# GpSimd adds the two key chunks of a head's last 132 queries, and the row sums on TensorE read 256 columns per head instead of 388

## The chip, the cores and the metric

The kernel runs on one core of a Trainium2 chip. The metric is device time in microseconds (us) of one execution. The engines are named as in the profile: PE is TensorE's matmul stream and PEld its weight loads, DVE is VectorE, ACT is ScalarE, POOL is GpSimd, and SP issues most of the DMAs.

## What is computed

A pre-norm transformer layer for 32 batches of 256 tokens of width 128, all in float32 at the interface. The attention has 16 heads of 64, rotary embedding, and 4 persistent keys and values in front of the 256 own ones, so each head has 260 keys. Cut to what matters here:

```python
scores = einsum('bhid,bhjd->bhij', q, k) * scale
scores = where(j <= i + 4, scores, min)          # i query, j key, 4 persistent keys
attn = softmax(scores, axis=-1)                   # exp, divided by its sum over the keys
out = einsum('bhij,bhjd->bhid', attn, v)          # then @ w_out.T and the residual
x = x + ffn(layernorm(x))                         # a gated scan over the batches
```

The step that the change touches is the sum over the keys in the softmax.

## The kernel before

**Tiles.** A batch has 8 pairs of heads, called s = 0 to 7. Keys lie on the 128 partitions in two chunks: chunk 0 holds keys 0 to 127 and meets all 256 queries; chunk 1 holds keys 128 to 255 and, by the causal mask, meets only queries 124 to 255 (Q1 = 124). The last four keys are handled apart in `prob_end`. So the exponentials of a head are 256 + 132 = 388 columns, and `prob` is `[128, 4 slots, 2 heads, 388]` in float32, with slot s % 4.

**Order of the work.** Every engine runs one outer loop over j and inside it eight steps s, an order written out by hand. Several batches are in flight: batch j is projected, batch j-1 goes through scores and attention, batch j-2 is normalised and projected out, batch j-3 goes through the feed-forward gates. In a step s the work runs as follows.

- PE: `project(j, s)` into the one bank `ps_proj` (L953), then work of other batches, `scores_for_max` (L985), `scores_t(j-1, s)` (L1007, L1010), `attend(j-1, s-1)` (L1044), and after it, where s is 2, 4, 7 and 0, the sums of four heads: `sums(j-1, 0)`, `sums(j-1, 1)`, `sums(j-1, 2)` and, in step 0 of the next j, `sums(j-2, 3)` (L1063). In steps 5 and 6 stands `project_out(j-2)`, four groups n = 0 to 3 (L1080), in step 3 and 7 a transpose of the row maxima (L993), and in step 0, right after `project(j, 0)`, `transpose_xn` (L1095).
- DVE: `rotate` (L752, L753), `maxima` (L763), in steps 4 and 5 the four `divide` (L799) that multiply by 1/sum, in step 6 `residual` (L804) and at its end `c_lo` (L843).
- SP: two DMAs that swap neighbouring partitions of `rope_b` into `rope_c`; in step 2 the DMAs that store 1/sum and spread it over the partitions (`linv_scratch`, `rinv`).
- POOL, the engine of the change: `rope_add(j, s-1)` (L385) waits for the swap's DMA; in step 7 `rstd(j-2)` (L393 to L399, four small operations on 2 columns); then `causal(j-1, s)`, two selects that zero what lies above the diagonal (L376, L378); in step 1 also `factors`.
- ACT: `exp(j-1, s)` (L521), `hi(j, s-1)` (L506, waits for `rope_add`), `raw_copy(j-1, s-1)` (L544), and in step 7, behind them, `second_norm(j-2)` (L600), which waits for `rstd` and whose result `xn` is what `transpose_xn` waits for.

**The sums.** Four heads r use four groups of 32 columns of the PE array at the same time. A float32 matmul is run as two instructions, so each chunk takes two rounds of four matmuls. The weights `ones_sum` are 1/256 in the column of the head's group.

Of the kernel before, what the change touches and what calls it, by code (L numbers as in the profile page):

```python
# [5 lines left out]
NB, NT, D = 32, 256, 128  # L6
NH, DH, NPM = 16, 64, 4
DI = NH * DH
P = 128
NPAIR = NH // 2  # L10
QT = NT // P
NKEY = NT + NPM
NEND = NKEY - 2 * P
Q1 = P - NPM
QE = NT - NEND
SCOL = NT + (NT - Q1)
CHUNKS = [(0, 0, 0), (1, Q1, NT)]
# [23 lines left out]
def wait(eng, sem, count):  # L41

    if isinstance(count, int) and count <= 0:
        return
    eng.wait_ge(sem, count)


def build(nc, x, x_last, w_qkv_t, w_out_t, norm_w, pm_k, pm_v, ffn_w, ffn_b, bo_row, consts_f32, consts_cast,
          out):
    f32, f16, bf16 = mybir.dt.float32, mybir.dt.float16, mybir.dt.bfloat16  # L50
    ALU = mybir.AluOpType
# [6 lines left out]
    with ctx:  # L58
        def sb(name, shape, dt):
            return ctx.enter_context(nc.sbuf_tensor(name, shape, dt))  # L60

        def sem(name):
# [62 lines left out]
        top = sb("top", [P, 2, QT, P], f32)  # L125
        masked = sb("masked", [P, 2, SW0 + NKEY], bf16)
        prob = sb("prob", [P, 4, 2, SCOL], f32)

# [15 lines left out]
        c2 = sb("c2", [P, NT], f32)  # L146
        c_hi = sb("c_hi", [P, NT], f16)
        c_lo = sb("c_lo", [P, NT], f16)
        cf = sb("cf", [P, QT * D], f32)
        linv_dram = nc.dram_tensor("linv_scratch", [2, 32, 2, NT], f32, kind="Internal").ap()  # L150
        v_end_dram = nc.dram_tensor("v_end_scratch", [P, DI], f32, kind="Internal").ap()

# [11 lines left out]
            "casts_act casts_dve casts_pool end_xn end_tr end_hi end_done ve_ready ve_copied ve_stored "  # L164
            "h_stats h_rstd h_xn h_tr h_hi_done h_lo_done "
            "qk_proj qk_read swapped0 swapped1 rope_sum hi_done sm_ready max_done top_tr top_copied "
            "st_ready exp_done causal_done pv_ready raw_done sum_ready linv_done linv_stored spread0 spread1 norm_done y_ready x1_done "
            "v_ready v_done v_end sx_done sx_rstd xn_ready xt_ready xt_hi_done xt_lo_done gate_ready gate_read c_hi_done state_done "
            "end_exp end_summed end_added k_end_done lin_ready pre_done cf_ready cf_done fin_sum fin_sum_pool fin_tanh fin_out fin_out_pool stored "
            "dve_tick pool_tick dve_pro dve_s dve_h dve_b dve_c pool_h pool_b").split()}  # L170
# [21 lines left out]
        def real(b):  # L192

            return not isinstance(b, int) or 0 <= b < NB
# [141 lines left out]
        @block.gpsimd  # L336
        def _(pool):
            G = nc.gpsimd
            G.memset(expo[:, :], -0.5).then_inc(S["casts_pool"], 1)
            G.memset(top[:, :, :, :], 0.0).then_inc(S["casts_pool"], 1)  # L340
            G.memset(h_hi[:, :, 0:NPM], 0.0).then_inc(S["casts_pool"], 1)
            G.memset(h_lo[:, :, 0:NPM], 0.0).then_inc(S["casts_pool"], 1)
            G.memset(bo_one[:, :], WS).then_inc(S["casts_pool"], 1)
            G.memset(eps[:, :], EPS_LN).then_inc(S["casts_pool"], 1)
            G.memset(minus[:, :], -1.0).then_inc(S["casts_pool"], 1)
            G.memset(one_e2[:, :], 1.0 + EPS_RMS).then_inc(S["casts_pool"], 1)
            G.memset(e1_e2[:, :], EPS_LN * EPS_RMS).then_inc(S["casts_pool"], 1)
            G.memset(prob_end[:, :, :, :, :], 0.0).then_inc(S["casts_pool"], 1)
            G.memset(prob_end_sum[:, :, :], 0.0).then_inc(S["casts_pool"], 1)
            G.memset(v_end[:, :], 0.0).then_inc(S["casts_pool"], 1)  # L350

            def factors(n, count, base):


                v, u = sh_mv[:, 0:n, 1], sh_u[:, 0:n]
                pool.wait_ge(S["h_stats"], count)
                G.tensor_tensor(u, v, one_e2[:, 0:n], ALU.mult).then_inc(S["pool_h"], 1)
                pool.wait_ge(S["pool_h"], base + 1)
                G.tensor_tensor(u, u, e1_e2[:, 0:n], ALU.add).then_inc(S["pool_h"], 1)
                G.tensor_tensor(sh_m[:, 0:n], sh_mv[:, 0:n, 0], minus[:, 0:n], ALU.mult).then_inc(S["pool_h"], 1)  # L360
                pool.wait_ge(S["pool_h"], base + 3)
                G.tensor_tensor(sh_r[:, 0:n], u, expo[:, 0:n], ALU.pow).then_inc(S["pool_h"], 1)
                pool.wait_ge(S["pool_h"], base + 4)
                G.tensor_tensor(sh_m[:, 0:n], sh_m[:, 0:n], sh_r[:, 0:n], ALU.mult).then_inc(S["h_rstd"], 1)

            pool.wait_ge(S["casts_pool"], 12)
            factors(QT + 1, 1, 0)

            def causal(bj, s):


                pool.wait_ge(S["exp_done"], NPAIR * bj + s + 1)
                G.sem_inc(S["pool_tick"], 1)
                c0 = prob[:, s % 4, :, 0:P]
                c1 = prob[:, s % 4, :, NT:NT + P]
                G.affine_select(out=c0, in_=c0, compare_op=ALU.is_ge, fill=0.0, base=NPM,  # L376
                                pattern=[[0, 2], [1, P]], channel_multiplier=-1)
                G.affine_select(out=c1, in_=c1, compare_op=ALU.is_ge, fill=0.0, base=0,  # L378
                                pattern=[[0, 2], [1, P]], channel_multiplier=-1).then_inc(S["causal_done"], 1)

            def rope_add(j, s):

                wait(pool, S["st_ready"], NPAIR * (j - 1) + s + 1)
                pool.wait_ge(swapped[s % 2], 32 * (NPAIR // 2 * j + s // 2 + 1))
                G.tensor_tensor(qk[:, s, :].rearrange("p (u n) -> p u n", u=2)[:, :, 0:NT],  # L385
                                rope_a[:, s % 4, :].rearrange("p (u n) -> p u n", u=2),
                                rope_c[:, s % 2, :].rearrange("p (u n) -> p u n", u=2),
                                ALU.add).then_inc(S["rope_sum"], 1)

            def rstd(cj):  # L390

                pool.wait_ge(S["sx_done"], cj + 1)
                G.tensor_tensor(sx_b[:, :], sx_mv[:, :, 1], eps[:, 0:QT], ALU.add).then_inc(S["pool_b"], 1)  # L393
                wait(pool, S["xn_ready"], cj)
                G.tensor_tensor(sx_m[:, :], sx_mv[:, :, 0], minus[:, 0:QT], ALU.mult).then_inc(S["pool_b"], 1)
                pool.wait_ge(S["pool_b"], 3 * cj + 2)
                G.tensor_tensor(sx_r[:, :], sx_b[:, :], expo[:, 0:QT], ALU.pow).then_inc(S["pool_b"], 1)
                pool.wait_ge(S["pool_b"], 3 * cj + 3)
                G.tensor_tensor(sx_m[:, :], sx_m[:, :], sx_r[:, :], ALU.mult).then_inc(S["sx_rstd"], 1)  # L399

            def body(j, p):
                a, b, c = real(j), real(j - 1), real(j - 2)
                for s in range(NPAIR):
                    if s == 0 and b:
                        rope_add(j - 1, NPAIR - 1)
                    if s >= 1 and a:
                        rope_add(j, s - 1)
                    if c and s == 7:
                        rstd(j - 2)
                    if b:  # L410
                        causal(j - 1, s)
                    if s == 1 and real(j + 1):
                        factors(QT, j + 2, POOL_H * (j + 1))

            iterations(nc.gpsimd, body)


            def fin_add(g):
                G.tensor_tensor(fin_pre(g), fin_pre(g), over_batches(cf[:, :]), ALU.add).then_inc(S["fin_sum_pool"], 1)

            def fin_res(g):
                pool.wait_ge(S["fin_tanh"], g + 1)
                G.tensor_tensor(fin_x(g), fin_x(g), fin_pre(g), ALU.add).then_inc(S["fin_out_pool"], 1)

            pool.wait_ge(S["cf_done"], 1)
            pool.wait_ge(S["x1_done"], NB)
            fin_add(FIN_POOL[0])
            for i in range(1, len(FIN_POOL)):
                fin_add(FIN_POOL[i])
                fin_res(FIN_POOL[i - 1])  # L430
            fin_res(FIN_POOL[-1])
# [479 lines left out]
        def _(pe):  # L911
# [142 lines left out]
            def sums(bj, g):  # L1054

                if g == 0:
                    wait(pe, S["linv_done"], bj)
                if g == 2:
                    wait(pe, S["x1_done"], bj)
                for kc, q0, c0 in CHUNKS:  # L1060
                    for r in range(4):
                        slot = (2 * g + r // 2) % 4
                        last = T.matmul(ps_sum[32 * r:32 * r + 32, q0:NT], ones_sum[:, g, :],  # L1063
                                        prob[:, slot, r % 2, c0:c0 + NT - q0],
                                        start=(g == 0 and kc == 0), stop=False, skip_group_check=True)
                if g == 3:
                    pe.wait_ge(S["end_summed"], bj + 1)
                    for r in range(4):
                        last = T.matmul(ps_sum[32 * r:32 * r + 32, QE:NT], ones_end[:, r % 2, 32 * r:32 * r + 32],
                                        prob_end_sum[:, r % 2, :], start=False, stop=True, skip_group_check=True)  # L1070
                last.then_inc(S["sum_ready"], 1)
# [244 lines left out]
```

## Time and profile before

| | |
|---|---|
| median of 3 runs | 1206.99 us (1204.7 to 1209.58) |
| the profiled execution, time | 1204.28 us |
| its span in the profile | 1202.5 us |
| PE busy | 1136.8 us (95%) |
| DVE busy | 942.5 us (78%) |
| ACT busy | 684.7 us (57%) |
| POOL busy | 655.0 us (54%) |

A time in the views below is counted from the start of the span. Between the span and the execution's own time lie 1.8 us. A busy PE is a modelled figure: matmuls overlap, so the start of the next one says more than the end of this one.

### The profile page before, as it was taken

The numbers are of one execution on the slowest core, as the hardware profiler recorded it, in microseconds if no ns is written. First come the engines' busy times: TensorE is split into PE (matmuls) and PEld (weight loads), VectorE is DVE, ScalarE is ACT, GpSimd is POOL, SyncE is SP. The second block draws the span as 40 slices with busy tenths as digits, with TensorE's granted clock in tenths as the row PEclk, the third lists the DMA queues.
The fourth block names the chain that finished last, engine by engine and source line by source line (L and its number), as shares of the span: only waits on it lengthen the run. The fifth ranks groups of instructions, "written<-read, shape, count | busy, mean of one in ns | idle before, by whom it ended". The sixth has DMA issues, their size and how long they took to land.

```text
span 1202.5 us, 36709 instructions
## 1 busy us (share of the span) xinstructions
PE 1136.8 (95%) x13099; PEld 802.8 (67%) x13099; DVE 942.5 (78%) x3302; ACT 684.7 (57%) x1474; POOL 655.0 (54%) x1082
## 2 busy tenths in 40 slices
PE   3889999999999999999999999999999999999981
PEld 2556767667776766777677677767667777766661
DVE  5677888888877888787878878877788878788636
ACT  3555565656555566655656665565555565565533
POOL 3544555556555555655555556555556556555425
PEclk8899999999999999999999999999999999999995
DMA  5222333332233333233333323333332333333204
GB/s 200 86 83 79 108 104 112 107 108 83 84 104 98 116 106 109 70 96 106 99 115 109 107 73 92 105 108 108 104 97 78 98 108 95 112 103 97 65 10 140
DMA packets 77990, 119.80 MB, mean 100 GB/s; under 512 B 13041, under 2 KB 35954, under 8 KB 77682
## 3 DMA queue, kind: packets, MB, share of 16 engines
q1 hardware_dynamic: 68722, 111.18, 30.7%
q10 hardware_dynamic: 9088, 6.29, 1.8%
q8 instruction: 105, 1.72, 0.6%
q14 instruction: 75, 0.61, 0.2%
HBM read 41.53 MB, written 8.78 MB: 42 GB/s over the span
## 4 chain that ended last, share of the span: by engine, by line
PE 76%; DVE 6%; DMA 5%; ACT 4%; issue 4%; POOL 3%; SPq 2%; DVEq 0%; ACTq 0%; POOLq 0%
PE bank_pv L1044 13%; PE bank_st L1007 12%; PE bank L953 12%; PE bank_sum L1080 8%; PE bank L971 6%; PE bank_sum L1063 6%; PE bank_sm L985 5%; DMA rope_c<-rope_b 4%; PE bank_st L1010 3%; PE bank L1166 2%; PE bank L1168 2%; ACT xn L600 2%; PE bank_sm L993 2%; POOL qk L385 2%; PE bank L1095 1%
## 5 line engine op out<-in xcount | busy, mean ns | idle before, releaser
L385 POOL TENSOR_TENSOR qk<-rope_a,rope_c 128x512 f32<-128x512 f32 x256 | 336.0, 1312 | 269.7 <-DMA rope_c<-rope_b 264.5
L763 DVE CUSTOM_DVE_ANT_0 masked<-bank_sm,mask_q 128x132 bf16<-128x132 f32 (+1 forms) x1024 | 307.6, 356 | 43.5 <-PE bank_sm L985 42.9
L521 ACT ACTIVATE prob<-bank_st 128x776 f32<-128x776 f32 x256 | 208.5, 814 | 160.0 <-PE bank_st L1010 159.2
L752 DVE TENSOR_TENSOR rope_a<-bank,cos 128x512 f32<-128x512 f32 x256 | 174.1, 680 | 125.1 <-PE bank L953 116.2
L1007 PE MATMUL bank_st<-qk 64*128 64x256 f32 (+1 forms) x2048 | 239.4, 326 | 0.1
L376 POOL TENSOR_SCALAR_AFFINE_SELECT prob<-prob 128x256 f32<-128x256 f32 x256 | 113.9, 445 | 227.5 <-ACT prob L521 226.4
L1044 PE MATMUL bank_pv<-prob,v_sb 128*64 128x256 f32 (+1 forms) x2048 | 224.7, 340 | 2.2 <-POOL prob L378 1.8
L506 ACT ACTIVATE qk_h<-qk 128x512 f16<-128x512 f32 x256 | 160.1, 625 | 98.0 <-POOL qk L385 96.9
L1007 PEld LDWEIGHTS bank_st<-qk 64*128 64x128 f32 x2048 | 154.8, 188 | 31.7 <-issue 0.8
L753 DVE TENSOR_TENSOR rope_b<-bank,sin 128x512 f32<-128x512 f32 x256 | 173.7, 679 | 0.0
L1044 PEld LDWEIGHTS bank_pv<-prob,v_sb 128*64 128x64 f32 x2048 | 124.5, 136 | 72.7 <-issue 31.4
L953 PE MATMUL bank<-h_hi,w_hi 128*128 128x256 f16 x512 | 143.7, 281 | 2.6 <-DVE rope_b L753 1.8
L953 PE MATMUL bank<-h_hi,w_lo 128*128 128x256 f16 x512 | 142.0, 277 | 0.0
L953 PE MATMUL bank<-h_lo,w_hi 128*128 128x256 f16 x512 | 141.8, 277 | 0.0
L1080 PE MATMUL bank_sum<-wo_sb,raw 128*128 128x128 f32 x1024 | 127.2, 277 | 3.2 <-DVE raw L799 3.2
L1080 PEld LDWEIGHTS bank_sum<-wo_sb,raw 128*128 128x128 f32 x1024 | 121.0, 192 | 11.8 <-DVE raw L799 9.0
L1010 PE MATMUL bank_st<-top_t,sel_shift 64*128 64x256 bf16 (+1 forms) x1024 | 126.4, 243 | 0.0
L378 POOL TENSOR_SCALAR_AFFINE_SELECT prob<-prob 128x256 f32<-128x256 f32 x256 | 116.5, 455 | 0.0
L1063 PE MATMUL bank_sum<-prob,ones_sum 128*32 128x256 f32 (+1 forms) x2048 | 110.6, 334 | 0.0
L553 ACT ACTIVATE v_sb<-bank 128x512 f32<-128x512 f32 x128 | 76.5, 597 | 59.5 <-PE bank L971 59.4
L799 DVE SCALAR_TENSOR_TENSOR raw<-rinv,raw 128x512 f32<-128x512 f32 x124 | 93.7, 796 | 5.7 <-DMA rinv<-linv_scratch 5.7
L544 ACT ACTIVATE raw<-bank_pv 128x256 f32<-128x256 f32 x256 | 94.9, 371 | 0.5 <-PE bank_pv L1050 0.5
(190 smaller groups left out, 1712.5 us busy)
## 6 DMA issues: line engine op xcount, KB each, us to landing
rope_c<-rope_b SPq DMA_DIRECT2D x512, 128.0 KB, 2.1
rinv<-linv_scratch SPq DMA_DIRECT2D x124, 256.0 KB, 4.5
out<-x_sb SPq DMA_DIRECT2D x16, 256.0 KB, 2.5
linv_scratch<-linv SPq DMA_DIRECT2D x62, 64.0 KB, 2.0
x_sb<-x ACTq DMA_DIRECT2D x28, 128.0 KB, 4.8
pre<-w_qkv_t ACTq DMA_DIRECT2D x1, 1024.0 KB, 5.5
v_sb<-pm_v SPq DMA_DIRECT2D x64, 8.0 KB
v_end<-v_end_scratch SPq DMA_DIRECT2D x64, 8.0 KB
```

The lines of the kernel that those rows point to most:

```text
L385: G.tensor_tensor(qk[:, s, :].rearrange("p (u n) -> p u n", u=2)[:, :, 0:NT], rope_a[:, s % 4, :].rearrange("p (u n) -> p u n", u=2), rope ...
L506: A.activation(qk_h[:, s, :].rearrange("p (u n) -> p u n", u=2)[:, :, 0:NT], qk[:, s, :].rearrange("p (u n) -> p u n", u=2)[:, :, 0:NT], A ...
L521: A.activation(prob[:, s % 4, :, :], ps_st[:, :, 0:SCOL], ACT.Exp).then_inc(S["exp_done"], 1)
L752: V.tensor_tensor(rope_a[:, s % 4, :], proj_bank(j, s)[:, :], cos[:, :], ALU.mult)
L753: V.tensor_tensor(rope_b[:, s % 2, :], proj_bank(j, s)[:, :], sin[:, :], ALU.mult).then_inc(S["qk_read"], 1)
L763: ins = V.tensor_tensor_reduce(masked[:, e, c0:c0 + n], ps_sm[:, e, c0:c0 + n], mask_q[:, c0:c0 + n], 1.0, LOWEST, ALU.add, ALU.max, top[: ...
L953: last = T.matmul(proj_bank(j, s)[:, u * NT:(u + 1) * NT], W[q][:, col:col + P], H[p][:, par, NPM:NKEY], start=(i == 0), stop=(i == 2))
L1007: T.matmul(ps_st[:, e, c0:c0 + NT - q0], qk[OWN[e], s, NT + kc * P:NT + (kc + 1) * P], qk[OWN[e], s, q0:NT], start=True, stop=False)
L1010: last = T.matmul(ps_st[:, e, c0:c0 + NT - q0], sel_shift[OWN[e], s, :], top_t[OWN[e], s // 4, q0:NT], start=False, stop=True)
L1044: last = T.matmul(ps_pv[OWN[e], q0:NT], v_sb[:, kc, col:col + DH], prob[:, s % 4, e, c0:c0 + NT - q0], start=(kc == 0), stop=(kc == 1))
L1063: last = T.matmul(ps_sum[32 * r:32 * r + 32, q0:NT], ones_sum[:, g, :], prob[:, slot, r % 2, c0:c0 + NT - q0], start=(g == 0 and kc == 0), ...
L1080: last = T.matmul(ps_sum[:, NT + q * D:NT + (q + 1) * D], raw[:, par, s, q * P:(q + 1) * P], wo_sb[:, s, :], start=(alone and s == 0 and q ...
```

## The change

`prob_add` is new on POOL, right behind `causal` in every step. It writes the sum of the two chunks for queries 124 to 255 into the new buffer `prob_2`, after a wait for the sums that last read the slot, and a wait for POOL's own selects. `sums` then runs two parts: queries 0 to 123 from `prob` (chunk 0 alone has keys for them), and queries 124 to 255 from `prob_2`. It waits for `prob_added`. The number of matmuls stays. `attend` still reads `prob`. `cf`, used only at the very end, is laid over `th` to make room.

```diff
+        prob_2 = sb("prob_2", [P, 4, 2, NT - Q1], f32)
...
-        cf = sb("cf", [P, QT * D], f32)
+        cf = th[:, 0, :]
...
+            def prob_add(bj, s):
+
+                wait(pool, S["sum_ready"], 4 * bj + (s - 4) // 2 + 1)
+                pool.wait_ge(S["causal_done"], NPAIR * bj + s + 1)
+                G.tensor_tensor(prob_2[:, s % 4, :, :], prob[:, s % 4, :, NT:SCOL], prob[:, s % 4, :, Q1:NT],
+                                ALU.add).then_inc(S["prob_added"], 1)
+
...
                     if b:
                         causal(j - 1, s)
+                        prob_add(j - 1, s)
...
-                for kc, q0, c0 in CHUNKS:
+                pe.wait_ge(S["prob_added"], NPAIR * bj + 2 * g + 2)
+                for part, (q0, q1) in enumerate(((0, Q1), (Q1, NT))):
                     for r in range(4):
                         slot = (2 * g + r // 2) % 4
-                        last = T.matmul(ps_sum[32 * r:32 * r + 32, q0:NT], ones_sum[:, g, :],
-                                        prob[:, slot, r % 2, c0:c0 + NT - q0],
-                                        start=(g == 0 and kc == 0), stop=False, skip_group_check=True)
+                        src = prob_2[:, slot, r % 2, :] if part else prob[:, slot, r % 2, 0:Q1]
+                        last = T.matmul(ps_sum[32 * r:32 * r + 32, q0:q1], ones_sum[:, g, :], src,
+                                        start=(g == 0 and part == 0), stop=False, skip_group_check=True)
```

## Rows read from the trace of the kernel before

**Rows 1.** The page's head: span, then busy time of each engine.

```profile
span 1202.5 us, 36709 instructions
PE 1136.8 (95%) x13099; PEld 802.8 (67%) x13099; DVE 942.5 (78%) x3302; ACT 684.7 (57%) x1474; POOL 655.0 (54%) x1082
```

**Rows 2.** Waits: engine and line waiting <- releaser: us in total, times, longest.

```profile
POOL qk L385 <- DMA rope_c<-rope_b: 264.5, 129, 8.4
POOL prob L376 <- ACT prob L521: 226.4, 157, 3.9
...
PEld bank L1095 <- ACT xn L600: 14.3, 31, 1.1
...
PEld bank_sum L1080 <- DVE raw L799: 9.0, 18, 0.8
...
PEld bank_pv L1044 <- POOL prob L378: 2.3, 3, 1.2
```

**Rows 3.** Groups of instructions by form: out<-in shapes xcount | busy us, mean ns.

```profile
L385 POOL TENSOR_TENSOR qk<-rope_a,rope_c 128x512 f32<-128x512 f32 x256 | 336.0, 1312 | 269.7 <-DMA rope_c<-rope_b 264.5 <-ACT prob L521 2.7 <-PE bank_st L1010 1.8
...
L378 POOL TENSOR_SCALAR_AFFINE_SELECT prob<-prob 128x256 f32<-128x256 f32 x256 | 116.5, 455 | 0.0
...
L1063 PE MATMUL bank_sum<-prob,ones_sum 128*32 128x256 f32 x1024 | 81.8, 391 | 0.0
...
L1063 PEld LDWEIGHTS bank_sum<-prob,ones_sum 128*32 128x32 f32 x2048 | 53.4, 109 | 40.4 <-issue 17.1
L1063 PE MATMUL bank_sum<-prob,ones_sum 128*32 128x132 f32 x1024 | 52.3, 276 | 0.0
```

**Rows 4.** Timeline of PE around the end of step 7: start us, us, what.

```profile
634.83 0.86 PE L1063 MATMUL bank_sum<-prob,ones_sum 128*32 128x256 f32 x16
635.63 0.28 PE L953 MATMUL bank<-h_hi,w_hi 128*128 128x256 f16 x1
...
636.18 0.27 PE L953 MATMUL bank<-h_lo,w_hi 128*128 128x256 f16 x1
636.56 0.44 PE L1095 MATMUL bank<-ident_f,xn 128*128 128x128 f32 x2
```

**Rows 5.** Timeline of POOL in the same steps 6 and 7.

```profile
631.90 0.41 POOL L378 TENSOR_SCALAR_AFFINE_SELECT prob<-prob 128x256 f32<-128x256 f32 x1
632.27 1.29 POOL L385 TENSOR_TENSOR qk<-rope_a,rope_c 128x512 f32<-128x512 f32 x1
...
634.12 0.71 POOL L397 TENSOR_TENSOR sx_r<-sx_b,expo 128x2 f32<-128x2 f32 x1
634.91 0.19 POOL L399 TENSOR_TENSOR sx_m<-sx_m,sx_r 128x2 f32<-128x2 f32 x1
```

**Rows 6.** Timeline of ACT in step 7 of the same batch.

```profile
634.13 0.82 ACT L521 ACTIVATE prob<-bank_st 128x776 f32<-128x776 f32 x1 [0.51 <-PE bank_st L1010]
...
635.37 0.38 ACT L544 ACTIVATE raw<-bank_pv 128x256 f32<-128x256 f32 x1
635.63 0.87 ACT L600 ACTIVATE xn<-x_sb,sx_m,sx_r 128x128 f32<-128x128 f32 x2
```

**Rows 7.** Timeline of DVE at the end of step 6, same batch.

```profile
632.58 1.26 DVE L843 SCALAR_TENSOR_TENSOR c_lo<-c,c_hi 128x256 f16<-128x256 f32 x1
```

**Rows 8.** All instructions of DVE line 843: duration ns min/median/max.

```profile
L843 DVE SCALAR_TENSOR_TENSOR c_lo<-c,c_hi x32: 390/1268/1373, 141.3 to 1178.5; 128x256 f16<-128x256 f32 x32
```

**Rows 9.** Timeline of POOL in steps 6 and 7, another batch.

```profile
806.16 0.41 POOL L378 TENSOR_SCALAR_AFFINE_SELECT prob<-prob 128x256 f32<-128x256 f32 x1
807.86 1.29 POOL L385 TENSOR_TENSOR qk<-rope_a,rope_c 128x512 f32<-128x512 f32 x1 [1.29 <-DMA rope_c<-rope_b]
...
810.32 0.20 POOL L399 TENSOR_TENSOR sx_m<-sx_m,sx_r 128x2 f32<-128x2 f32 x1
```

**Rows 10.** Timeline of PE in that batch, step 0 of the next j.

```profile
811.48 0.44 PE L1095 MATMUL bank<-ident_f,xn 128*128 128x128 f32 x2 [0.76 <-ACT xn L600]
```

**Rows 11.** Timeline of POOL, ACT and DVE in steps 4 and 5, an early batch.

```profile
200.76 1.28 POOL L385 TENSOR_TENSOR qk<-rope_a,rope_c 128x512 f32<-128x512 f32 x1 [4.01 <-DMA rope_c<-rope_b]
...
202.07 0.63 ACT L506 ACTIVATE qk_h<-qk 128x512 f16<-128x512 f32 x1 [2.75 <-POOL qk L385]
...
203.37 0.48 DVE L698 SCALAR_TENSOR_TENSOR h_lo<-bank,nw,h_hi 128x256 f16<-128x256 f32 x1 [1.34 <-ACT h_hi L460]
```

More of the change, by code:

```diff
@@ L166, in build @@
             "qk_proj qk_read swapped0 swapped1 rope_sum hi_done sm_ready max_done top_tr top_copied "
-            "st_ready exp_done causal_done pv_ready raw_done sum_ready linv_done linv_stored spread0 spread1 norm_done y_ready x1_done "
+            "st_ready exp_done causal_done prob_added pv_ready raw_done sum_ready linv_done linv_stored spread0 spread1 norm_done y_ready x1_done "
             "v_ready v_done v_end sx_done sx_rstd xn_ready xt_ready xt_hi_done xt_lo_done gate_ready gate_read c_hi_done state_done "
```

## The prediction

> **What bounds the kernel now.** I read the page's head first: PE is busy for 95% of the span, DVE for 78%, POOL for 54% [rows 1]. PE's stream is therefore what has to get shorter, and a shorter stream is worth its full length only where PE is not about to wait for something. So the next view is the waits. POOL waits 264.5 us for the swap's DMA and 226.4 us for the exponentials [rows 2]: 491 us over 256 steps, 1.9 us per step, so on average it has room. PE itself waits for little, but one entry comes back in 31 of the 32 batches: the weight load of `transpose_xn` (L1095) waits for `xn` from ACT, 14.3 us in all. A second, `project_out` behind `divide`, comes in 18 batches or groups, 9.0 us; the third, `attend` behind the selects, has 3 cases and 2.3 us [rows 2]. In each batch there are thus one or two places at which another chain is as long as PE's own. What the change is worth is decided there. For the first place I went to the timelines of one ordinary batch [rows 4 to 7] and of one in which POOL was late [rows 9, 10].
>
> **What PE saves.** A group of sums is four rounds of four matmuls, now of 256, 256, 132 and 132 columns, then of 124, 124, 132 and 132. A group and what follows it lie 0.80 us apart (634.83 to 635.63) [rows 4]. A matmul of 256 columns lasts 391 ns, one of 132 columns 276 ns [rows 3]; the fixed part is the same, so a shortened round gives back 115 ns, two of them 0.23 us. A round can also not be shorter than the weight load of the next, 109 ns [rows 3], which holds 124 columns at about the price of 132 and leaves a little more in the first round. I take 0.22 us a group, between 0.20 and 0.23. There are 2048 / 16 = 128 groups: 28 us gross, 2.3%, or 0.88 us a batch. The added wait for `prob_added` costs nothing in itself: the last add needed by `sums` comes one whole step ahead of it, as the select does now, and the selects stop PE 3 times only [rows 2].
>
> **What the add costs on POOL.** No row shows it. A TENSOR_TENSOR on 512 columns takes 1312 ns on average [rows 3] and 1.28 us undisturbed [rows 11]; one on 2 columns takes 0.19 [rows 5]. That is 2.1 ns a column, and for 2 x 132 = 264 columns 0.19 + 0.55 = 0.75 us (rounded). The bounds: not below a select on 256 columns, 0.455 us [rows 3], and not above the 512-column add, 1.31 us. The nearest by kind, two inputs, is the latter, and the line between 2 and 512 columns carries the 0.75. The wait for POOL's own selects is priced as the one in `rstd`: L397 ends at 634.83 and L399 starts at 634.91, 0.08 us [rows 5]. So 0.83 us are inserted after each `causal`, 212 us in all, and POOL comes to about 867 us, 72%. In most steps the 1.9 us of waiting cover it.
>
> **Where it is not covered: step 7.** After `causal(6)` ends (631.90 + 0.41 = 632.31) POOL starts `rope_add(6)` at once (632.27) and then `rstd`, which ends at 634.91 + 0.19 = 635.10 [rows 5]. ACT could start `xn` from then on, and does at 635.63, behind `raw_copy` [rows 6]. PE's projection has its last matmul at 636.18 and `transpose_xn` starts at 636.56 [rows 4]; it waits for `xn`. How much later may `rstd` be? The other batch answers. There the swap was late, `rope_add` began 807.86 - 806.57 = 1.29 us after the select, `rstd` ended at 810.52, 3.95 us after the select instead of 2.79, and PE stood 0.76 us before L1095 [rows 9, 10] instead of 636.56 - 636.45 = 0.11 [rows 4]. So 1.16 us more on POOL became 0.65 us on PE: the slack is 0.51 us. With the add in between, `rope_add` starts about 0.80 us later. A second thing happens there: `c_lo` on DVE, with two inputs in SBUF, asks at 632.58 and lasts 1.26 us, to just after the end of `rope_add` [rows 7]; alone it takes 0.39 [rows 8]. The two engines shut each other out. In the new order either `rope_add` goes first, and `rstd` ends 0.80 + 2.83 = 3.63 us after the select (2.83 is 635.10 - 632.27), or `c_lo` slips in for the rest of its work, about 0.28 us with what overlaps taken off 0.14, and then it is 0.83 + 0.14 + 2.66 = 3.63 again (2.66 is the late batch's 810.52 - 807.86). Both are 0.84 us over the 2.79 of now. Less 0.51 of slack, `transpose_xn` is 0.33 us late in each batch. The work of `xn` starts from `exp(7)`, which itself waits for the scores (634.13, 0.51 <-PE) [rows 6], that is, from a point before `sums(2)`. So the 0.22 us that `sums(2)` saves in step 7 only lengthens the wait for `xn` and is lost in every batch.
>
> The Trainium skill ("SBUF — State Buffer", who interferes with whom) says that a VectorE instruction with two SBUF inputs and a GpSimd instruction that reads SBUF exclude each other for the whole instruction; the trace agrees, with 390 ns against a median of 1268 ns for the same line [rows 8]. By this rule the new add would also hold up `divide`, which is priced as a rival below.
>
> **Where it is half covered: steps 4 to 6.** `rope_add(3)` waits 4.01 us for a swap that queues behind the spreading of 1/sum; ACT waits 2.75 us for it, and DVE 1.34 us for `h_hi` behind that [rows 11]; then come `maxima`, `divide` and `project_out`. This chain starts from the inverse in step 1, before `sums(0)` and `sums(1)`. PE waited for a `divide` 18 times [rows 2]; I count these as 18 batches in which the chain is as long as PE's stream, and there the 0.44 us of `sums(0)` and `sums(1)` are lost too. In the other 13 they are kept. What POOL adds does not lengthen this chain: the add after `causal(3)` lies inside the 4.01 us.
>
> **The sum.** 13 batches keep three groups and pay the delay: 0.66 - 0.33 = 0.33 us gained each, 4.3 us. 18 keep one group: 0.22 - 0.33 = 0.11 us lost each, 2.0 us. The last batch gives 0.2. The span goes from 1202.5 to about 1200 us, the profiled execution from 1204.28 to 1201.8, and the median of the runs, 2.7 us above it, from 1206.99 to 1204.5 us. The smaller buffer for `cf` moves nothing: it is written after the last batch. A measurement of this kernel can tell about 0.5%, 6 us, from no change.
>
> **Rivals.**
>
> 1. *The gain comes through.* The chain in steps 4 to 6 has slack that the 18 waits hide (they are short), or the add is cheaper. With the delay of 0.33 and three groups kept in all 31 batches it is 31 x 0.33 = 10 us: 1197. If the add costs only the lower bound, 0.455, the insertion is 0.54 and the delay 0.04: 31 x 0.62 = 19 us, 1188. For it: POOL's large idle time. Against it: the idle time is not in step 7 [rows 5]. Chance 0.32.
> 2. *POOL's chain takes over in step 7: slower.* The mean gain that can be kept is (13 x 0.66 + 18 x 0.22) / 31 = 0.40 us a batch; the delay passes that once the insertion is above 0.83 + 0.07 = 0.90 us. At the upper bound, 1.31 + 0.08 = 1.39 us, the delay is 0.89 and the loss 31 x 0.49 = 15 us: 1222. At 1.0 us for the add it is 0.18 x 31 = 6 us, 1213. For it: PE waits at this place in all batches already. Against it: the line through two sizes gives 0.75. Chance 0.15.
> 3. *The add shuts out `divide`.* If one add of 0.75 us stands ahead of the last `divide` in step 5 in the 18 tied batches, `project_out` is that much later: 18 x 0.75 = 13 us less the 2 us gained, 1218. Against it: after `causal(4)` there is `rope_add` in the same place already, and a shorter instruction may even help. Chance 0.08.
> 4. *About even*, the forecast: 0.45.
>
> **How the numbers follow.** The time is that of the likeliest case, 1204.5 us; its own range is 1201 to 1212. For 8 in 10 I reach down to 1190, which takes in most of rival 1, and up to 1217, which leaves out the upper bound of the add. Faster by over 0.5%: 0.32; within it: 0.45; slower: 0.15 + 0.08 = 0.23.
>
> **What would show it.** In the profile of the changed kernel: the 256-wide form of L1063 gone and a 124-wide one at about 275 ns; a new POOL group x256 at about 750 ns; POOL near 867 us; the idle time of PE before the transposes of `xn` up from 0.11 to about 0.11 + 0.33 + 0.22 = 0.66 us in an ordinary batch, with POOL's last `rstd` operation named behind it through ACT; the waits of `project_out` for `divide` in no fewer batches and longer. The prediction is wrong if the new group lies far from 750 ns, if the wait before L1095 does not grow, or if PE waits in a new place, such as before `sums`.

## The result

The changed kernel takes 1226.5 us in the median against 1208.3 us of the kernel before: a ratio of 1.015, 95% interval 1.012 to 1.018. It is 18 us slower, where I had forecast about 3 us faster and a range up to 1217. The profiled execution took 1225.42 us, with a span of 1223.7 us.

### The profile page after: what moved, and what is told of

The parts are those of the page before. It is cut to its first block, busy times and chain, and to the rows that moved or that the text cites. A ratio compares the mean times of both kernels' runs of the same rounds, so it can differ in the third digit from the quotient of the medians.

```text
span 1223.7 us, 37279 instructions
## 1 busy us (share of the span) xinstructions
PE 1111.0 (91%) x13099; PEld 799.5 (65%) x13099; DVE 952.4 (78%) x3302; ACT 683.5 (56%) x1474; POOL 845.7 (69%) x1338
## 4 chain that ended last, share of the span: by engine, by line
PE 52%; POOL 21%; ACT 9%; DVE 7%; issue 6%; DMA 3%; SPq 1%; POOLq 0%; ACTq 0%; DVEq 0%
PE bank_st L1016 9%; PE bank_sum L1090 9%; PE bank_pv L1053 7%; PE bank L962 7%; POOL qk L393 7%; PE bank_sm L994 4%; ACT prob L530 4%; POOL prob L386 3%; PE bank L980 3%; PE bank_sum L1074 2%; PE bank_st L1019 2%; POOL prob L377 2%; POOL sx_r L405 2%; POOL sh_r L363 2%; DMA rope_c<-rope_b 2%
## 5 line engine op out<-in xcount | busy, mean ns | idle before, releaser
L393 POOL TENSOR_TENSOR qk<-rope_a,rope_c 128x512 f32<-128x512 f32 x256 | 336.5, 1314 | 96.6 <-DMA rope_c<-rope_b 90.6
L377 POOL TENSOR_SCALAR_AFFINE_SELECT prob<-prob 128x256 f32<-128x256 f32 x256 | 119.5, 467 | 194.2 <-ACT prob L530 194.1
L386 POOL TENSOR_TENSOR prob<-prob 128x264 f32<-128x264 f32 x256 | 191.1, 746 | 38.3 <-POOL prob L379 1.0
L379 POOL TENSOR_SCALAR_AFFINE_SELECT prob<-prob 128x256 f32<-128x256 f32 x256 | 121.1, 473 | 0.0
L994 PE MATMUL bank_sm<-qk_h 64*128 64x132 f16 (+1 forms) x1024 | 88.4, 251 | 34.3 <-ACT top_t L544 30.8
L808 DVE SCALAR_TENSOR_TENSOR raw<-rinv,raw 128x512 f32<-128x512 f32 x124 | 107.3, 906 | 5.9 <-DMA rinv<-linv_scratch 5.9
```

What stands on the lines that cost most here:

```text
L386: G.tensor_tensor(prob_2[:, s % 4, :, :], prob[:, s % 4, :, NT:SCOL], prob[:, s % 4, :, Q1:NT], ALU.add).then_inc(S["prob_added"], 1)
```

## The profile after

The head of the page, with busy times, and two groups of section 5:

```profile
span 1223.7 us, 37279 instructions
PE 1111.0 (91%) x13099; PEld 799.5 (65%) x13099; DVE 952.4 (78%) x3302; ACT 683.5 (56%) x1474; POOL 845.7 (69%) x1338
...
L386 POOL TENSOR_TENSOR prob<-prob 128x264 f32<-128x264 f32 x256 | 191.1, 746 | 38.3 <-POOL prob L379 1.0
...
L808 DVE SCALAR_TENSOR_TENSOR raw<-rinv,raw 128x512 f32<-128x512 f32 x124 | 107.3, 906 | 5.9 <-DMA rinv<-linv_scratch 5.9
```

PE is busy 25.8 us less than in [rows 1], and the span is 21.2 us longer: PE stands idle for some 47 us more. The new POOL group costs 746 ns each (its tile `prob_2` appears as `prob`, buffer numbers left out), and POOL, with 69%, is far from full. `divide` grew from a mean of 796 ns to 906; whether the add does that is asked below. The shortened matmuls, by form:

```profile
L1074 PE MATMUL bank_sum<-prob,ones_sum 128*32 128x124 f32 x1024 | 53.6, 281 | 0.0
L1074 PE MATMUL bank_sum<-prob,ones_sum 128*32 128x132 f32 x1024 | 52.3, 276 | 0.0
```

Busy time fell by 81.8 - 53.6 = 28.2 us [rows 3]. Where the 47 us went is in the view of the waits, and it names two lines (the lines of the kernel after are some 10 higher; L994 is `scores_for_max`, L1105 `transpose_xn`):

```profile
POOL qk L393 <- DMA rope_c<-rope_b: 90.6, 54, 8.4
...
PEld bank L1105 <- ACT xn L609: 32.9, 31, 1.9
...
PE bank_sm L994 <- ACT top_t L544: 30.8, 30, 2.1
PE bank L1105 <- ACT xn L609: 24.3, 31, 1.6
```

The line of L994 is as good as new: PE waits once per batch, 1.03 us each, before `scores_for_max` for ACT's copy of the row maxima (`copy_top`). In the view of before the same wait is 0.8 us, in one case. The last line is the place I had looked at. There the matmul's own waits were 2.9 us in 4 cases in the kernel before; they are 24.3 us in 31 now. The sum, 30.8 + 24.3 - 2.9 = 52 us, less the 28 us saved, is 24, against a span longer by 21. POOL's wait for the swap's DMA fell from 264.5 us [rows 2] to 90.6: the add used up idle time in most steps, as planned. One thing went against my forecast: the weight loads of `project_out` wait for `divide` 10 times, 5.2 us, and not 18 times or more [rows 2].

**The place that I missed.** First POOL in steps 1 and 2 of a batch:

```profile
620.17 0.41 POOL L379 TENSOR_SCALAR_AFFINE_SELECT prob<-prob 128x256 f32<-128x256 f32 x1
620.72 0.74 POOL L386 TENSOR_TENSOR prob<-prob 128x264 f32<-128x264 f32 x1
621.42 0.20 POOL L358 TENSOR_TENSOR sh_u<-sh_mv,one_e 128x2 f32<-128x2 f32 x1
...
622.90 0.19 POOL L365 TENSOR_TENSOR sh_m<-sh_m,sh_r 128x2 f32<-128x2 f32 x1
623.28 1.27 POOL L393 TENSOR_TENSOR qk<-rope_a,rope_c 128x512 f32<-128x512 f32 x1 [0.18 <-issue]
```

Then ACT, and PE, in the same stretch:

```profile
622.48 0.82 ACT L530 ACTIVATE prob<-bank_st 128x776 f32<-128x776 f32 x1 [0.36 <-PE bank_st L1019]
624.58 0.63 ACT L515 ACTIVATE qk_h<-qk 128x512 f16<-128x512 f32 x1 [1.28 <-POOL qk L393]
625.12 0.37 ACT L553 ACTIVATE raw<-bank_pv 128x256 f32<-128x256 f32 x1
625.38 0.87 ACT L600 ACTIVATE xn<-x_sb,sh_m,sh_r 128x128 f32<-128x128 f32 x2
626.15 0.37 ACT L544 ACTIVATE top_t<-bank_sm 128x256 bf16<-128x256 f32 x1
...
626.66 0.34 PE L994 MATMUL bank_sm<-qk_h 64*128 64x132 f16 x4 [1.18 <-ACT top_t L544]
```

In step 1 POOL has three things to do on end: the selects, now the add, and `factors` (621.42 to 623.09). Only then comes `rope_add(1)`, whose swap has landed: it starts at 623.28 with "issue" before it, not a DMA. `hi(1)` on ACT waits for it 1.28 us, and ACT works in order: `raw_copy`, `first_norm` and `copy_top` all move with it. `scores_for_max(0)` of step 3 cannot overwrite the bank of the maxima until `copy_top` has read it, so PE stands 1.18 us. The same stretch in the kernel before had ACT waiting already, with nothing of it on PE:

```profile
611.88 1.27 POOL L385 TENSOR_TENSOR qk<-rope_a,rope_c 128x512 f32<-128x512 f32 x1 [0.17 <-issue]
...
613.18 0.63 ACT L506 ACTIVATE qk_h<-qk 128x512 f16<-128x512 f32 x1 [0.39 <-POOL qk L385]
...
614.75 0.36 ACT L535 ACTIVATE top_t<-bank_sm 128x256 bf16<-128x256 f32 x1
...
615.26 0.34 PE L985 MATMUL bank_sm<-qk_h 64*128 64x132 f16 x4
```

`copy_top` ended at 615.11 and PE came at 615.26: the slack was gone before the change. The 0.39 us of waiting was the sign, a row that I had not read. It is no accident of this batch: it stands in all 30 batches where these steps meet, mostly as 0.18 us, 7.7 us in sum, and in none of them did the `rope_add` behind `factors` wait for its swap. In the kernel after, the same waits are mostly 1.06 us, 35.0 us in sum: the whole insertion, some 0.88 us, is passed on to ACT.

**The place that I foresaw.** POOL, ACT, DVE and PE at the end of steps 6 and 7, against [rows 4 to 7]:

```profile
643.08 0.41 POOL L379 TENSOR_SCALAR_AFFINE_SELECT prob<-prob 128x256 f32<-128x256 f32 x1
643.64 0.74 POOL L386 TENSOR_TENSOR prob<-prob 128x264 f32<-128x264 f32 x1
644.34 1.47 POOL L393 TENSOR_TENSOR qk<-rope_a,rope_c 128x512 f32<-128x512 f32 x1
...
646.98 0.19 POOL L407 TENSOR_TENSOR sx_m<-sx_m,sx_r 128x2 f32<-128x2 f32 x1
...
647.21 0.88 ACT L609 ACTIVATE xn<-x_sb,sx_m,sx_r 128x128 f32<-128x128 f32 x2 [0.28 <-POOL sx_m L407]
...
643.75 0.91 DVE L852 SCALAR_TENSOR_TENSOR c_lo<-c,c_hi 128x256 f16<-128x256 f32 x1
...
646.01 0.65 PE L1074 MATMUL bank_sum<-prob,ones_sum 128*32 128x124 f32 x16
646.59 0.28 PE L962 MATMUL bank<-h_hi,w_hi 128*128 128x256 f16 x1
...
648.14 0.44 PE L1105 MATMUL bank<-ident_f,xn 128*128 128x128 f32 x2 [0.72 <-ACT xn L609]
```

`rstd` ends at 647.17, 3.68 us after the select (643.49); I had 3.63. `c_lo` was shut out by the add, ran before `rope_add` and stretched that to 1.47 us. A group of sums takes 0.58 us to the next work (646.01 to 646.59) instead of 0.80. PE stands 0.72 us before the transposes; I had 0.66.

## The experiments

Each ratio is against runs of the kernel before from the same session, whose median was 1207.2 us in the first session (up to the single adds), 1210.4 in the second (the moves) and 1208.7 in the third (the controls and the single groups). Compare kernels of different sessions by their ratios.

**The gain and the cost apart.** First the shorter sums with no add, from the changed kernel. The part of chunk 0 for the late queries is then missing from the row sums, so the output is wrong and only the time counts:

```diff
-                        prob_add(j - 1, s)
...
-                pe.wait_ge(S["prob_added"], NPAIR * bj + 2 * g + 2)
...
-                        src = prob_2[:, slot, r % 2, :] if part else prob[:, slot, r % 2, 0:Q1]
+                        src = prob[:, slot, r % 2, NT:SCOL] if part else prob[:, slot, r % 2, 0:Q1]
```

> No add on POOL; the sums read chunk 0 for queries 0 to 123 and chunk 1 alone for queries 124 to 255, so the part of chunk 0 for the late queries is left out of the row sums. This is the gain without the cost. Theory A (the gain of one group in four is lost before the transposes of xn, and the chain of steps 4 to 6 is not in the way): 31 x 0.66 = 20 us faster, about 1187. Theory B (the chain of steps 4 to 6 takes the gain of two more groups in 18 batches): 12 us, about 1196.

Measured: 1195.1 us, ratio 0.990 (0.987 to 0.993). That is 12 us faster, the figure of theory B. Of 28 us taken out of PE's stream, 12 arrive. The waits of this kernel show where most of the rest went, PE's own having been 2.9 us at `transpose_xn` and 3.2 at `project_out` before; L1103 is `transpose_xn`, L1088 `project_out`:

```profile
PEld bank L1103 <- ACT xn L608: 21.3, 31, 1.4
PEld bank_sum L1088 <- DVE raw L807: 16.3, 27, 0.8
PE bank L1103 <- ACT xn L608: 12.6, 31, 1.1
PE bank_sum L1088 <- DVE raw L807: 7.3, 19, 0.5
```

The weight load of `project_out` waits for `divide` 27 times now, 18 times before [rows 2].

Then the add with the sums as before; it keeps `prob_add` and the wait and puts the old loop over CHUNKS back:

```diff
                 pe.wait_ge(S["prob_added"], NPAIR * bj + 2 * g + 2)
-                for part, (q0, q1) in enumerate(((0, Q1), (Q1, NT))):
+                for kc, q0, c0 in CHUNKS:
...
```

> The add and its wait stay, the sums read 388 columns as before. The cost without the gain. Theory A (two places: the add of step 1 through factors, first_norm and copy_top to scores_for_max in step 3, and the add of step 6 through rstd to xn): in the changed kernel PE stood 30.8 us at the first and 24.3 at the second, with 0.22 us a batch of PE's own saving in each; so (1.03 - 0.22) + (0.78 - 0.22 - 0.11) = 1.26 us a batch, 39 us, about 1247. Theory C (the add hurts by shutting out DVE's two-input work, all over): the same sum of about 39, but with the time lost before project_out.

Measured: 1237.5 us, ratio 1.025 (1.022 to 1.028), 30 us slower instead of 39. The two parts add up: -1.0% + 2.5% = +1.5%, the change as measured. Theory A had the places right, and the waits too: 24.3 us at `top_t` and 16.8 at `xn`, 37 more than before. Its time was too high, because other waits of PE got shorter, by some 4 us in the views (the one of `project_out` for `divide` from 3.2 to 0.3).

**Which of the eight adds.** The sums as before, and `prob_add` in one step only, step 1 in the kernel shown and step 6 in the other; `sums` waits for that one add alone:

```diff
-                        prob_add(j - 1, s)
+                        if s in (1,):
+                            prob_add(j - 1, s)
...
```

> The sums as before, and the add only in step 1 of each batch (its result is not used). Theory A: 0.8 us a batch at scores_for_max of step 3, 25 us, about 1233, and the idle time of PE before L985's successor line up from 4 to about 29 us. Theory C: an eighth of the cost, 5 us, about 1213.

Measured: 1226.2 us, ratio 1.016 (1.013 to 1.018): 19 us from 32 adds, where theory A had 25 and theory C 5.

> The sums as before, and the add only in step 6. Theory A: 0.45 us a batch before the transposes of xn, 14 us, about 1222. My prediction's own figure for this place, 0.33, gives 10 us, 1218. Theory C: 5 us, about 1213.

Measured: 1218.2 us, ratio 1.010 (1.006 to 1.014): 11 us, close to the 10 of my prediction. Together the two give 1.55% + 1.00% = 2.55%, and all eight adds gave 2.52%. By the three intervals that is good to about half a per cent, some 6 us: the other six adds cost nothing that can be measured here. Theory C, that the add hurts by shutting out DVE, falls. `divide` runs in steps 4 and 5, and its mean was 913 ns in the kernel with an add in step 1 alone, and 846 in the one with shorter sums and no add. With all eight adds and the two moves below it was 774, less than the 796 of the kernel before. So the mean does not follow the adds beside it. In each kernel PE's new wait is at its own place, first the add in step 1, then that in step 6:

```profile
PE bank_sm L995 <- ACT top_t L545: 23.6, 30, 1.6
...
PE bank L1108 <- ACT xn L610: 2.4, 5, 0.9
```

```profile
PE bank L1108 <- ACT xn L610: 17.6, 31, 1.4
```

**Taking the cost away by order alone.** The whole change, with one thing moved on POOL.

```diff
-                    if s == 1 and real(j + 1):
+                    if s == 0 and real(j + 1):
                         factors(QT, j + 2, POOL_H * (j + 1))
```

> The whole change, with factors moved on POOL from the end of step 1 to the end of step 0, so that rope_add(1) in step 2 is no longer behind select, add and factors together. Theory A: the 19 us that the add of step 1 cost by itself come back, 1226.5 - 19 = 1207, and PE's 30.8 us of waits for top_t fall to nothing; the 24.3 us before the transposes of xn stay. Theory D (any 0.8 us more on POOL costs its share wherever it stands): the time stays near 1226.

Measured: 1204.3 us, ratio 0.994 (0.992 to 0.996). The change alone was at 1.015, so 2.1%, some 25 us, came back, more than the 19 that the add of step 1 had cost by itself. The waits for `top_t` would also have eaten the gain of `sums(0)`, up to 7 us, which fits; it was not tested by itself. PE's wait for `top_t` is down from 30.8 us in 30 cases to 1.4 in 4.

```diff
-                        prob_add(j - 1, s)
+                        if s == 7:
+                            prob_add(j - 1, 6)
+                        if s != 6:
+                            prob_add(j - 1, s)
```

> The whole change, with the add of step 6 moved behind rope_add, rstd and the selects of step 7. Theory A: the 11 us of the add of step 6 come back, about 1215, and the wait for xn falls to what the shorter sums alone leave, 12.6 us. Theory D: near 1226.

Measured: 1215.2 us, ratio 1.003 (1.001 to 1.005). By the ratios 1.2%, some 14 us, came back, where theory A had 11. PE's wait for `xn` is 13.1 us, near the 12.6 of the kernel without adds. Theory D falls: it is not how much POOL does, but what stands behind it.

> Both moves together. Theory A: all 30 us come back and the gain without the cost is left, about 1196, as the kernel with shorter sums and no add at all had (1195). Theory D: near 1226; if the other six adds cost something that the single ones hid, between 1200 and 1210.

Measured: 1196.0 us, ratio 0.988 (0.985 to 0.990). All eight adds are in, the output is complete, and the time is that of the kernel with no add at all (0.990, 0.987 to 0.993). The cost is gone. `divide` in this kernel, and in the one with the add of step 1 alone:

```profile
L811 DVE SCALAR_TENSOR_TENSOR raw<-rinv,raw 128x512 f32<-128x512 f32 x124 | 91.0, 774 | 5.7 <-DMA rinv<-linv_scratch 5.7
```

```profile
L809 DVE SCALAR_TENSOR_TENSOR raw<-rinv,raw 128x512 f32<-128x512 f32 x124 | 108.2, 913 | 5.9 <-DMA rinv<-linv_scratch 5.9
```

**Is the rest of the gain held at xn?** To both moves, one on ACT:

```diff
+                    if s == 7 and c:
+                        second_norm(j - 2)
                     if s >= 1 and b:
                         raw_copy(j - 1, 1 - p, s - 1)
...
-                    if s == 7 and c:
-                        second_norm(j - 2)
```

Between the two places stand `first_norm` and `state_high`, which run in other steps.

> Both moves, and on ACT second_norm ahead of raw_copy in step 7, so that xn starts about 0.26 us earlier, when the exponential's follower hi(6) is through. If the wait for xn still takes the gain of one group in four, this gives 31 x 0.26 = 8 us more than both, about 1188. If attend(7) comes to wait for raw_copy instead, no more than both.

Measured: 1190.0 us, ratio 0.982 (0.980 to 0.984), the fastest kernel of the study. PE's waits:

```profile
PEld bank L1108 <- ACT xn L612: 16.3, 31, 1.5
PEld bank_sum L1093 <- DVE raw L811: 16.2, 22, 1.0
...
PE bank L1108 <- ACT xn L612: 6.4, 8, 1.2
```

The wait for `xn` is 6.4 us in 8 cases instead of 15.4 in 31 with both moves alone.

As controls, on the kernel before, the move of `second_norm` and the move of `factors`, each alone:

> The kernel before, with only second_norm ahead of raw_copy on ACT in step 7. PE's own idle time before the transposes of xn was 2.9 us there, 0.11 a batch below what a row shows: 1 to 5 us faster if the start of xn was the bound, nothing otherwise.

Measured: 1203.3 us, ratio 0.9945 (0.993 to 0.996): 6.6 us by the ratio, 5.4 by the medians, at the upper end of what was expected or above it. This gain has nothing to do with the change, and it is as large as the one just seen (0.988 to 0.982). So the question of the heading is answered with no: the shorter sums are worth 1.2% without this move and 1.3% with it (0.982 against 0.9945), and the rest of their 28 us does not come free when `xn` starts earlier.

> The kernel before, with only factors moved from step 1 to step 0. PE did not wait for top_t there, so theory A expects no change (within 2 us). A gain of several us would mean that the recovery in the kernel with both moves was not the add's cost but a gain of its own.

Measured: 1208.9 us, ratio 1.000 (0.998 to 1.002). Moving `factors` is worth nothing in the kernel before; on the shorter sums without the add it was not tried.

**Which groups' saving arrives.** No add, and only some groups shortened, with the same part of the sums left out there; g = 2 in the kernel shown, g = 0 and 1 in the other:

```diff
...
+                short = g in (2,)
+                for part, (q0, q1) in enumerate(((0, Q1 if short else NT), (Q1, NT))):
...
```

> No add on POOL; only the group of sums of step 7 (g = 2) reads the shorter columns, and leaves out chunk 0 for the late queries. Theory A: its 0.22 us a batch, 7 us in all, are lost before the transposes of xn: no change, 0 to 1 us. Theory E (the wait for xn does not swallow it): 6 to 7 us faster, a ratio of 0.9945.

Measured: 1207.1 us, ratio 0.998 (0.996 to 0.999): about 3 us of 7 by the ratio, with 1 to 5 inside the interval, where I had 0 to 1. PE's wait for `xn` rose from 2.9 us to 13.5, in 31 cases. That is more than the whole saving, so this row shows the place and not the amount: part of the saving is swallowed there, not all.

> The same for the groups of steps 2 and 4 alone (g = 0 and 1). Theory B (the chain of inverse, DMA, rope_add, divide in steps 4 to 6 holds in 18 of 31 batches): 13 x 0.44 = 6 us faster, ratio 0.995. Theory E: 31 x 0.44 = 14 us, ratio 0.989.

Measured: 1206.1 us, ratio 0.998 (0.996 to 0.999): 3 us of 14, less than both theories. The chain of steps 4 to 6 seems to hold in more batches than I had counted; the weight loads of `project_out` (L1089) waited 29 times, their matmuls 22 times:

```profile
PEld bank_sum L1089 <- DVE raw L807: 18.3, 29, 0.8
...
PE bank_sum L1089 <- DVE raw L807: 8.6, 22, 0.5
```

So the 12 us of the shorter sums agreed with theory B in the total, and its count of 18 batches was not borne out. The group of step 0 (g = 3) was not run alone. Which of the chain's links (the store of 1/sum, its spread, the late swap, `hi` and `h_high` on ACT) would have to be shorter was not tried.

## Why the prediction was wrong

- **What PE saves: right.** 0.22 us a group was measured (0.80 to 0.58), 28.2 us of busy time in all, as forecast.
- **The price of the add: right.** 746 ns against 0.75 us. POOL came to 846 us, I had 867: my sum counted the 0.08 us of waiting before each add as busy time. Without them it is 655 + 192 = 847.
- **Step 7: right.** 0.72 us before the transposes against 0.66, with `c_lo` slipping in between as one of the two orders had it, and the add of step 6 alone costs 11 us against the 10 that 0.33 us in 31 batches make.
- **Steps 4 to 6 and the gain that can be kept: right in sum, in part by luck.** The shorter sums alone bring 12 us; by my count it was 13 x 0.66 + 18 x 0.22 = 12.5. The parts were off both ways: of the group in step 7 about 3 us of 7 arrive, where I had none, and of the two groups before it 3 us of 14, where I had 6. In the changed kernel the waits of `project_out` for `divide` became fewer (10 after 18), where I had expected no fewer. PE comes later there, having waited for `top_t` in step 3: with `factors` moved, and that wait gone, they are 21 again, 15.2 us.
- **The step that failed** is the sentence "In most steps the 1.9 us of waiting cover it." I took an average over all steps, looked at step 7, where I had seen a wait on PE, and priced the rest at nothing but for a word on `causal(3)`. Behind the add of step 1 POOL had no waiting at all: `factors` stood between the selects and `rope_add(1)`, and ACT already waited for the latter in every batch, 0.39 us in the one shown and 0.18 in most. The add made that 1.06 us, and PE came to wait for what ACT does next; PE waiting in a new place was among my own signs of being wrong. This missed place is the largest cost of the change, 19 us alone and some 25 with what it ate of the gain. With it the forecast of 2.5 us faster becomes, in a sum made afterwards, 1202.5 - 2.5 + 19 = 1219 us of span, and 1225 with the 25; 1223.7 was measured.
- **The rivals.** Rival 2, POOL's chain taking over, is what happened in kind, but I had placed it in step 7 alone and made it hang on a dearer add. The upper end of the range, 1217, came from that and so did not hold the missed place. Rival 3, the add shutting out `divide`, is not borne out: the six other adds, among them those of steps 4 and 5, cost nothing that can be measured, and the 906 ns against 796 are not theirs, since `divide` took 913 with no add near it and 774 with all eight. Rival 1 was not reached; the kernel with the new order comes near it.

## What to carry to other kernels

POOL was idle for 46% of the span and yet had no room where its instructions stand back to back. Before adding work in every step of a pipeline, list for each step what follows the added work in that engine's queue and what released it: "issue" or the engine's own work before it means that the full price is passed on to whoever waits for it. Then follow it through the in-order queue of each engine that waits, down to the bank or buffer that the busiest engine needs. A consumer that already waits for the engine is the sign. Here ACT waited for `rope_add` 96.9 us in 69 cases in the kernel before, and 30 of these, though short, were at the place that I missed. What an add costs can sometimes be undone by order alone: here the same work, with two moves, went from 1.5% slower to 1.2% faster.

## What the runs showed of the hardware

- Between the end of the select and the start of the add, which has two waits in front of it, lay 0.15 us (643.49 to 643.64), not the 0.08 between two small operations with one wait [rows 5].
- The Trainium skill ("SBUF — State Buffer", who interferes with whom) says that a VectorE instruction with two SBUF inputs contends with a GpSimd instruction that reads SBUF. The trace agrees: `c_lo` took 0.91 us beside the add, 0.39 alone [rows 8].
- New to me was that the one that waits seems to get its turn between two instructions of the other. `c_lo` ended at 644.66, 0.28 us after the end of the add (644.38), so its work fell into the start of `rope_add`, which took 1.47 us instead of 1.27. The median of `c_lo` is 906 ns in this kernel and 1268 in the kernel before, where it waited for the end of a `rope_add` [rows 7, 8].
- The mean time of `divide` ran from 773 to 933 ns over these kernels without following the adds: 846 ns with the shorter sums and no add (ratio 0.990), 774 ns with all eight adds and both moves (ratio 0.988).
